# Attention block with conditional layer norms: the normalisation of the attention output moved from token layout to the transposed layout

## The reference

```python
B, N, D = 16, 256, 256            # 16 heads of 16 channels
h = sln(hidden, w)                # gamma * layernorm(h) + beta, gamma and beta from w
qkv = (h @ Wqkv.T + bqkv).reshape(B, N, num_heads, hd, 3)
q, k, v = [jnp.moveaxis(qkv[..., i], 2, 1) for i in range(3)]
energy = jnp.einsum('bhqd,bhkd->bhqk', q, k)
att = jax.nn.softmax(energy, axis=-1) / D ** 0.5
out = jnp.einsum('bhqk,bhkd->bhqd', att, v)
out = jnp.moveaxis(out, 1, 2).reshape(B, N, D)
h1 = out @ Wp.T + bp + hidden
return sln(h1, w) + h1
```

## Time and profile before

| | before |
|---|---|
| median of 3 runs | 345.17 us (344.89 to 345.49) |
| the profiled execution | 345.56 us |
| its span, first to last instruction | 343.8 us |
| TensorE busy | 332.5 us, 97% |
| VectorE busy | 298.3 us, 87% |
| ScalarE busy | 242.8 us, 71% |
| GpSimd busy | 159.1 us, 46% |
| SP's queue of transfers | 46.74 MB, 49.2% of 16 engines |

### The profile page before, as it was taken

How to read it: one execution, slowest core, us unless ns; L and a number is a source line. 1 busy time by engine, 2 the same in 40 slices (tenths; PEclk the granted TensorE clock), 3 DMA queues, 4 the chain that set the end, 5 groups by cost and what they waited for, 6 DMA issues and landing times.

```text
span 343.8 us, 8981 instructions
## 1 busy us (share of the span) xinstructions
PE 332.5 (97%) x3173; PEld 286.8 (83%) x3173; DVE 298.3 (87%) x728; ACT 242.8 (71%) x476; POOL 159.1 (46%) x187
## 2 busy tenths in 40 slices
PE   8888999999999999999999999999999999999993
PEld 4677879888888988888888988888898988888773
DVE  4888978799898989899898989989898988999684
ACT  7664876868676786868686876868687786766740
POOL 5765544437164545527264644617254643224330
PEclk9999999999999999999999999999999999999999
DMA  7396445456555454555545454655556354652021
GB/s 242 126 218 186 124 115 140 129 155 157 170 141 156 134 152 135 173 156 170 142 125 169 134 155 134 184 142 160 161 135 157 98 157 123 182 146 67 16 61 61
DMA packets 47705, 48.87 MB, mean 142 GB/s; under 512 B 6287, under 2 KB 41374, under 8 KB 47662
## 3 DMA queue, kind: packets, MB, share of 16 engines
q1 hardware_dynamic: 44494, 46.74, 49.2%
q10 hardware_dynamic: 1184, 1.07, 1.2%
q0 software_dynamic: 1984, 0.51, 0.8%
HBM read 9.99 MB, written 4.23 MB: 41 GB/s over the span
## 4 chain that ended last, share of the span: by engine, by line
PE 87%; DVE 5%; DMA 3%; ACT 1%; issue 1%; ACTq 1%; SPq 0%; DVEq 0%
PE m L976 24%; PE st L976 19%; PE sa L976 18%; PE pv L976 17%; PE pv L1065 4%; DVE mx L692 3%; PE pv L1146 2%; PE m L1105 2%; DMA wqkv<-WqkvT_dram 2%; DMA kst<-qk_l 1%; PE pv L1079 1%; PE m L1079 1%; ACT p L602 0%; DVE qk_l L727 0%; ACTq L625 0%
## 5 line engine op out<-in xcount | busy, mean ns | idle before, releaser
L692 DVE TENSOR_REDUCE mx<-sa 128x2 f32<-128x512 f32 x256 | 171.5, 684 | 28.4 <-PE sa L976 27.3
L602 ACT ACTIVATE p<-st 128x512 f32<-128x512 f32 x240 | 140.9, 598 | 37.5 <-PE st L976 33.2
L976 PE MATMUL sa<-kst,qst 126*128 126x256 f32 x512 | 105.6, 288 | 2.0 <-DMA kst<-qk_l 1.0
L976 PE MATMUL st<-qst,kst 128*128 128x256 f32 x496 | 104.1, 292 | 0.2
L976 PEld LDWEIGHTS st<-qst,kst 128*128 128x128 f32 x496 | 75.1, 188 | 13.8 <-issue 12.8
L976 PEld LDWEIGHTS sa<-kst,qst 126*128 126x128 f32 x512 | 78.6, 189 | 4.6 <-DVE mx L692 1.7
L368 POOL DMA_DIRECT2D qst<-m_h x31 | 17.6, 567 | 112.4 <-DVE m_l L701 112.4
L976 PE MATMUL pv<-p,v_st 128*32 128x256 f32 x1008 | 61.0, 382 | 0.0
L976 PEld LDWEIGHTS pv<-p,v_st 128*32 128x32 f32 x1008 | 29.5, 109 | 21.0 <-ACT p L602 1.5
L976 PE MATMUL m<-hT_h,wqkv_h 128*128 128x256 f32 x128 | 36.8, 300 | 1.3 <-ACT hT_h L616 0.7
L377 POOL TENSOR_SCALAR xn<-xa,mv,rstd 128x256 f32<-128x256 f32 x28 | 34.2, 1227 | 1.5
(11 more groups left out here) (149 smaller groups left out, 566.2 us busy)
## 6 DMA issues: line engine op xcount, KB each, us to landing
qst<-qk_h SPq DMA_DIRECT2D x64, 128.0 KB, 2.4
qst<-qk_l SPq DMA_DIRECT2D x64, 128.0 KB, 2.5
kst<-qk_h SPq DMA_DIRECT2D x62, 128.0 KB, 2.5
kst<-qk_l SPq DMA_DIRECT2D x62, 128.0 KB, 2.8
xa<-x_dram SPq DMA_DIRECT2D x16, 256.0 KB, 3.0
gb<-gb_rows SPq DMA_DIRECT2D x16, 256.0 KB, 3.9
out_dram<-y SPq DMA_DIRECT2D x15, 256.0 KB, 3.4
wqkv<-WqkvT_dram SPq DMA_DIRECT2D x1, 512.0 KB, 5.6
```

Of the source, the lines that this page charges most:

```text
L602: nc.scalar.activation(p32[:, h, :], st_ps[h % 2][:], ACT.Exp).then_inc(exp_done, 1)
L692: dve.tensor_reduce(mx[:, par(a), h // HH, (h % HH) * TT:(h % HH + 1) * TT], sa_ps[h % 2][:].rearrange("p (t n) -> p t n", t=TT), AX.X, AL ...
L976: return nc.tensor.matmul(o, l, r, start=start, stop=stop)
```

## The change

For batches 0 to 13 (`by_transfer`) the attention output stays in the transposed layout.

- `v_st` has values and constants in turn, so the even rows of `oT` are values and the odd rows sums.
- SP moves the even rows of each half of `oT` to 64 rows of `o_rows` (128 KB), and one sum row of each head to `sums`, as 128 rows of 32 numbers (`send_out`).
- VectorE takes the reciprocals of `sums`, 128x32, in one instruction (`reciprocal`, slot 7).
- SP gathers them into 16 rows of 512 (`gather_rec`, two transfers) and then spreads each row over eight partitions (`spread_rec`, 256 KB, all within SBUF).
- VectorE multiplies both halves, 128x512, in one instruction (`normalise`, ahead of slot 11's maximum).
- ScalarE rounds it in slot 12, GpSimd makes the remainder behind its own `low_h` (slot 13); `low_h` now waits for `normalise`.
- The twelve transposes a batch are gone. The output projection has its 12 products ordered so that `aT_l` is needed for the last four only, in slots 13, 14, 15 and 15. `Wp` and the value bias are permuted on the host to the new row order.
- The statistics of x (`norm1`) move from slots 4 and 5 to slots 12 to 14, for the batch after. Slot 14 instead of 12 evicts g = 0.
- Batches 14 and 15 go by tokens as before; in the tail the transposes of both halves of `att` come after the last heads' normalisation.

```diff
-Q_SLOTS, K_SLOTS, V_SLOTS, P_SLOTS = (0, 1, 3, 4), (4, 5, 5, 6), (7, 7, 8, 8), (12, 13, 14, 15)
+Q_SLOTS, K_SLOTS, V_SLOTS, P_SLOTS = (0, 1, 3, 4), (4, 5, 5, 6), (7, 7, 8, 8), (13, 14, 15, 15)
-S_O1, S_O0 = 3, 12
+S_O1, S_O0 = 3, 14
...
+            def send_out(a, g):
+                if not by_transfer(a):
+                    return
+                half_rows = slice(g * P // 2, (g + 1) * P // 2)
+                sp.wait_ge(oT_ready, 2 * a + g + 1)
+                wait(sp, recs_in, 32 * a)
+                sp.dma_start(sums[half_rows, :], oT[1:P:32, g, :]).then_inc(sums_in[g], 16)
+                wait(sp, aTh_ready, a)
+                wait(sp, aTl_ready, a)
+                sp.dma_start(o_rows[half_rows, :], oT[0:P:2, g, :]).then_inc(o_in[g], 16)
+            def gather_rec(a):
+                sp.wait_ge(rec_ready, a + 1)
+                for n in range(2):
+                    sp.dma_start(recs[n:2 * HH:2, :], sums[:]).then_inc(recs_in, 16)
+            def spread_rec(a):
+                sp.wait_ge(recs_in, 32 * (a + 1))
+                wait(sp, rows_ready, a)
+                sp.dma_start(o_rec, recs.rearrange("r (d n) -> r d n", d=1)
+                             .broadcast_to([2 * HH, HD // 2, 2 * N])).then_inc(rec_in, 16)
...
                 for t in range(2):
                     for low in range(2):
                         send(a, g, t, low)
+                        if g == 0 and t == 0 and low == 0:
+                            spread_rec(a - 3)
...
+            def low_att(a):
+                wait(pool, aTh_ready, a + 1)
+                pool.tensor_tensor(aT_l[:].rearrange("p k n -> p (k n)"), o_rows[:],
+                                   aT_h[:].rearrange("p k n -> p (k n)"), ALU.subtract).then_inc(aTl_ready, 1)
...
                     if h == 12:
+                        wait(pool, rows_ready, min(b, B - 2))
                         low_h(b + 3)
+                    if h == 13 and by_transfer(b - 1):
+                        low_att(b - 1)
...
-                    if h == S_AT + 1 and has(b - 1):
-                        wait(act, attT_done, 1 * (b - 1) + 1)
+                    if h == S_AH and has(b - 1):
+                        wait(act, rows_ready, 1 * (b - 1) + 1)
...
+            def reciprocal(a):
+                for g in range(2):
+                    wait(dve, sums_in[g], 16 * (a + 1))
+                dve.reciprocal(sums[:], sums[:]).then_inc(rec_ready, 1)
+            def normalise(a):
+                for g in range(2):
+                    wait(dve, o_in[g], 16 * (a + 1))
+                wait(dve, rec_in, 16 * (a + 1))
+                dve.tensor_tensor(o_rows[:], o_rows[:], o_rec, ALU.mult).then_inc(rows_ready, 1)
...
+                    if n == 0:
+                        wait(pe, aTh_ready, a + 1)
+                    if n == 8:
+                        wait(pe, aTl_ready, a + 1)
...
-                    if h == S_AT and has(b - 1):
-                        turn_att(b - 1)
...
-                    if h == S_OT1:
-                        out_by_token(b - 1, 1)
-                    if h == S_OT0:
+                    if h == 14 and b == B - 2:
                         out_by_token(b, 0)
```

More of the change, by code:

```diff
@@ L310, in step @@
                     stack(b + 1, 1)
+                send_out(b - 1, 1)
                 if has(b + 4) and has(b):
@@ L314, in step @@
                     sp.dma_start(xbuf(b + 4), x_t[b + 4]).then_inc(x_in[(b + 4) % 4], 16)
+                gather_rec(b - 1)
                 if has(b):
                     stack(b + 2, 0)
+                if not has(b + 2):
+                    spread_rec(b - 1)
                 if first(b + 1):
@@ L702, in low_max @@
                                          in1=m_h[:, g, :], op0=ALU.mult, op1=ALU.subtract).then_inc(ml_ready, 1)
-            def normalise(a, g, stage):
-                if not has(a):
+            def reciprocal(a):
+                if not by_transfer(a):
                     return
[L708 to L717, removed]
+                for g in range(2):
+                    wait(dve, sums_in[g], 16 * (a + 1))
+                dve.reciprocal(sums[:], sums[:]).then_inc(rec_ready, 1)
@@ new lines, in normalise, with normalise_tokens @@
+            def normalise(a):
+                if not by_transfer(a):
+                    return
+                for g in range(2):
+                    wait(dve, o_in[g], 16 * (a + 1))
+                wait(dve, rec_in, 16 * (a + 1))
+                dve.tensor_tensor(o_rows[:], o_rows[:], o_rec, ALU.mult).then_inc(rows_ready, 1)
+            def normalise_tokens(a, g):
+                n = 2 * (a - B + 2) + g + 1
+                by_head = pv_ps[g][:].rearrange("p (t h d) -> p t h d", t=TT, h=HH)
+                wait(dve, o_done, n)
+                dve.reciprocal(rec[:, g], by_head[:, :, :, 1:2]).then_inc(rec_tokens, 1)
+                wait(dve, rec_tokens, n)
+                wait(dve, attT_done, a - B + 2)
+                for t in range(TT):
+                    o = dve.tensor_tensor(att[:, t, :].rearrange("p (c g j d) -> p g c j d", c=2, g=2, j=HH // 2)[:, g],
+                                          by_head[:, t, :, 0:VC:2].rearrange("p (c j) d -> p c j d", c=2),
+                                          rec[:, g, t].rearrange("p (c j) d -> p c j d", c=2)
+                                          .broadcast_to([P, 2, HH // 2, HD]), ALU.mult)
+                o.then_inc(att_ready, 1)
@@ L1224, in finish @@
             def finish():
-                wait(pe, att_ready, 2 * B - 1)
-                for t in range(TT):
-                    o = nc.tensor.transpose(sa_ps[1][:, t * P:(t + 1) * P], att[:, t, 0:P], ident[:])
-                o.then_inc(aT0_done, 1)
+                pe.wait_ge(att_ready, 3)
                 for c, bank in ((0, sa_ps[0]), (1, pv_ps[0])):
```

125 lines of the change are left out of this document (75 added, 50 removed).

## The result

| | before | after |
|---|---|---|
| median | 345.09 us (4 runs) | 405.51 us (402.13 to 406.98, 4 runs) |
| profiled execution, its span | 345.56, 343.8 us | 402.13, 400.3 us |
| ratio to before | | 1.1735 (95% interval 1.1651 to 1.182) |

The forecast was 341.0, faster, with a range of 331 to 350. The change costs 60 us, and the time lies outside the range.

A forecast was written before the change was run, and what follows sets the result against it. TensorE's queue was taken as the bound: removed transposes save 1.32 us a batch, less 1.0 of stall, over 14 batches gains 4.5, less 0.3 in the tail, from 345.56 to 341.4, so 341.0 against the median; range 331 to 350.

The forecast's parts named there:

- rival (a): Reciprocals in time for `normalise`: stall 0.2 to 0.4 us a step, gain 13 to 15, time 331 to 333; chance 0.20.
- The offset of the spread's issue: On SP's queue, the spread is issued 2.8 us behind the first gather, at 11.9 against 9.1.
- the gather's landing: The second gather of reciprocals lands 2.1 us after its issue, bounds 1.9 and 2.5.
- I take 2.65, with 2.3 and 3.9 as bounds: Landing time in us of the 256 KB spread within SBUF, from its issue to its arrival for `normalise`.
- bound by `gb`: Upper bound of 3.9 us for the spread, from a load of one source row into many partitions, from memory outside.
- t: Offset in the step at which VectorE's `normalise` starts, forecast 14.6, set by the late reciprocals; VectorE itself arrives at 14.0.
- D: TensorE's stall per step behind the late `normalise`: its start offset less 13.8, so 0.8 us, taken as 1.0 in all.
- rival (b): Slower because the spread is late: break-even where the stall reaches 1.3 us; 348 or 355 us; chance 0.25.
- 0.15 a step on average: Hold-ups of SP's issues: about one of 0.9 us a step, four of 23 issues on the path, 0.15 us on average.
- Seven more issues ... that still fits, by half a microsecond: SP's queue goes from 19 to 26 issues, 16.6 us in a 19.2 us step, plus a 2.1 us wait.
- at no cost: Moving the statistics of x to slots 12 to 14 costs nothing; GpSimd uses them only in the next step's slot 5.
- The chance of 0.25 for slower: Probability given to the change making the kernel slower, against 0.68 for faster and 0.07 for the same.

The follow-up runs named there:

- e8: The changed kernel without the spread, as e6, and with the statistics of x behind the maxima of slots 0 and 1: 334.69 us, ratio 0.9684.
- e6: The changed kernel with the spread left out, `normalise` waiting for the gather alone, output not normalised: 337.57 us, ratio 0.9726.
- e2: The changed kernel with the spread reading all 128 partitions of `wb`, so not the reciprocals: 355.87 us, ratio 1.0291.
- e3: The changed kernel with the spread reading eight overlapping windows of each of partitions 0 to 15, no row repeated, values no reciprocals: 404.55 us, ratio 1.1692.
- e4_warm: The changed kernel with sixteen products of zeros added in slot 13 ahead of the waiting score product: 382.19 us, ratio 1.1048.
- e1: The changed kernel with the 16 rows of reciprocals on partitions 0, 8, ..., 120 instead of 0 to 15: 365.08 us, ratio 1.0551.
- v4: v3 with four of its eight sends (k, heads 0 to 7) issued by ScalarE in slots 9, 10, 12 and 13: 378.36 us, ratio 1.0908.
- v7: v4 with SP's load of gb and the output (256 KB each) moved to the end of the step: 351.88 us, ratio 1.0193.
- v3: The changed kernel with e1's rows, `normalise` in slot 14, projection in next step's slots 0 and 1, statistics behind maxima of slots 0 and 1: 361.37 us.
- e7: e5 with the statistics of x behind the maxima of slots 0 and 1 instead of slots 12 to 14: 347.03 us.
- e5: e1 with the reciprocal earlier on VectorE, ahead of slot 5's `qk_l`: 346.91 us, ratio 0.9946.

## Why the prediction was wrong

**What held.** TensorE's queue was the bound, and the transposes are worth having out: without the spread the kernel takes 334.7 to 337.6 (e8, e6), against 331 to 333 of rival (a). The offset of the spread's issue, 2.78 behind the gather's (2.8), the gather's landing, 2.2 (2.1), and the order of who waits for whom (`normalise` for the spread, TensorE for the maximum of slot 13) were right. A step of e2 with the priced landing ran at 14.67 and 19.07, less the 0.50 of the low clock at its start: as worked out.

**The step that failed: "I take 2.65, with 2.3 and 3.9 as bounds".** The spread took 5.3. The price came from rows 7 by bytes: an x load of 256 KB and a send of 128 KB. An x load writes all 128 partitions, and a send reads all 128 and writes 16 at a stride of eight. The spread reads 16 neighbouring ones, and no row of before did with more than 8 KB. Its bound by `gb` was drawn for another reason (one source row into many), which within SBUF costs nothing, as e3 shows. Put 5.30 into the prediction's own sum: t = 11.9 + 5.30 + 0.05 = 17.25, D = 3.45 + 0.2 = 3.65, 14 x (3.65 - 1.32) + 0.3 = 32.9, so 378.5. e4_warm, with that wait and the clock held up, ran at 382.2. The mechanism is rival (b)'s and its formula was good to 4 us; its bound was not.

**A term that was missing: the granted clock.** The sum took a stall at its length. A stall of some 3 us was followed by 3.2 us at half the rate in the step shown; it cost 1.7 us a step and 23 us in all (e4). Before, TensorE never paused, so no row showed it. The Trainium skill (TensorE: Matmul & The Clock Gate, Part 1: The HAM clock gate) describes a gate that throttles an engine that has been idle; the trace agrees, with 0.43 for pairs of 0.24 behind the idle stretch.

**A term that was too small: "0.15 a step on average" for hold-ups.** With the landing of e1 (3.4) the prediction's sum gives t = 15.35, D = 1.75 and 351.9; measured 365.1. With e2's 2.7 it gives 342; measured 355.9. So some 13 us, about 0.9 a step, come from elsewhere. Part is the clock again (0.975 in e1). Part are the spreads beside a packet of the instruction queue: six in each profiled execution, 1.8 us longer on average than the others in e2 and 0.8 in e1, so up to 11 and 5 us if TensorE waits for all of it. And the hold-ups of issues by which the prediction priced this term are of the same kind: all four that it saw between 184 and 250 in rows 6 have such a packet in flight. It took them for a delay of SP's issues alone, spread evenly over them (and divided by 23 issues where it counts 26 elsewhere, which changes little), and had no term for a transfer that lands late beside them. v4 against v7 shows besides that transfers in flight together slow each other, by 0.9 us on a 128 KB send.

**"Seven more issues ... that still fits, by half a microsecond".** It did in the changed kernel, where no slot 0 waits for a send for long. It did not once the projection took slots 0 and 1 and the reciprocal stayed in slot 7 (v3): 1.0 to 1.2 us of waiting for the last send in each step.

**Statistics "at no cost".** Priced at nothing; e8 against e6 has 1.5 to 3 us, with overlapping intervals, and e7 against e5 nothing beyond the scatter. Not settled.

The 60 us are thus: about 33 by the late spread (worked out), 23 by the clock behind it (e4) and 4 for the rest. The hold-ups, some 13 us in e1 and e2, leave so little here. The trace of the changed kernel has a reason: this spread is no later beside a packet of the instruction queue: it takes 4.6 to 5.6 us with one and 5.1 to 5.5 without. The chance of 0.25 for slower was too low, since one unknown row carried the whole forecast and its upper bound was taken from a row that differed in what mattered.

## What to carry to other kernels

Price a transfer by the partitions that it reads and writes, and not by its bytes alone. A compact intermediate on 16 neighbouring partitions cost 2.6 us more than the same bytes from all 128; rows at a stride of eight gave back 1.9 of it with one index changed. And where an engine has never paused, a stall on it can cost more than its length: look for what the clock does behind it. Before a new transfer goes into a stretch, count what is in flight there, on every queue, that of the instructions too. Where a median hides two groups, as in e2, look at them step by step.

## What the runs showed of the hardware

- 256 KB within SBUF landed in 5.3 us from partitions 0 to 15, in 3.4 from 0, 8, ..., 120, and in 2.7 from all 128; whether a row is read once or eight times made no difference (5.3 both).
- Behind a stall of 3 us or so TensorE ran at its 1.2 GHz level (0.51 granted over 3.1 us); sixteen products of zeros within the stall avoided it (mean clock 0.916 without and 0.994 with them).
- One packet of 16 KB on the instruction queue went with a spread of 3.7 to 4.8 us instead of 2.3 to 2.8 (e2, 6 of 14 steps), and with pairs of SP's issues of 1.6 us or more instead of 1.2 (10 of 10 before, 11 of 11 in e2).
- Issuing sends from a second engine's queue did not make them land sooner (the remainders of k in 4.1 us in v4); moving 512 KB of other transfers away did (3.2).
- A reciprocal of 128x32 took 0.34 us, one of 128x16 0.248.
